# A two-turn engine loop written out, and a one-column sum of squares, in a fused hybrid block on one core

## The reference, cut to what matters

```python
x = x + attn_a(layernorm(x))   # gated recurrence over time, 8 heads, state 64 x 128 per head
x = x + ffn(layernorm(x))      # x @ ternary(weight).T * alpha + bias
x = x + attn_b(layernorm(x))   # softmax attention across the 8 sequences, 16 heads of 8
x = x + ffn(layernorm(x))      # the same weights as above
```

```python
y = y * rsqrt(mean(y * y, axis=-1) + 1e-6) * rms_weight     # y is 512 wide
return y @ out_proj_w.T
```

## Time and profile before

| what | us |
|---|---|
| median of 3 runs | 606.64 (604.37 to 607.63) |
| the profiled execution's own time | 608.52 |
| its span, from the first to the last instruction | 606.8 |
| mean granted TensorE clock in it | 0.966 of full speed |
| busy: PE, DVE, ACT, POOL | 526.3, 470.1, 482.5, 433.8 |

### The profile page before, as it was taken

How to read it: one execution, slowest core, us unless ns; L and a number is a source line. 1 busy time by engine, 2 the same in 40 slices (tenths; PEclk the granted TensorE clock), 3 DMA queues, 4 the chain that set the end, 5 groups by cost and what they waited for, 6 DMA issues and landing times. The chain is left out here.

```text
span 606.8 us, 13457 instructions
## 1 busy us (share of the span) xinstructions
PE 526.3 (87%) x3932; PEld 437.9 (72%) x3932; DVE 470.1 (77%) x1093; ACT 482.5 (80%) x1478; POOL 433.8 (71%) x568
## 2 busy tenths in 40 slices
PE   5978999999999898896999888899998786879287
PEld 4866888888887777785887777788777575766175
DVE  6666576687659999983767999997559979953995
ACT  3799999999998879695998887789999789843101
POOL 7348777878777887783678796977768876944742
PEclk9989999999999999997999999999999989987769
DMA  8841222132111112231111111232211112000001
GB/s 198 219 112 50 75 74 81 59 99 76 59 44 52 59 59 59 62 102 35 56 59 59 59 53 31 93 94 93 88 31 54 63 41 66 27 18 2 1 0 36
DMA packets 52309, 39.44 MB, mean 65 GB/s; under 512 B 7301, under 2 KB 48010, under 8 KB 52234
## 3 DMA queue, kind: packets, MB, share of 16 engines
q1 hardware_dynamic: 45898, 35.39, 19.7%
q10 hardware_dynamic: 6336, 3.15, 1.8%
HBM read 33.44 MB, written 4.46 MB: 62 GB/s over the span
## 5 line engine op out<-in xcount | busy, mean ns | idle before, releaser
L937 ACT ACTIVATE turned<-ps,sct 128x128 f32<-128x128 f32 x376 | 110.7, 446 | 0.0
L922 ACT ACTIVATE turned<-ps,sct 128x128 f32<-128x128 f32 x368 | 103.3, 434 | 6.4 <-DMA sct<-packed 3.9
L1282 DVE TENSOR_TENSOR_SCAN lmat<-arow,band 128x512 f32<-128x512 f32 x64 | 86.5, 1356 | 5.6 <-POOL band L651 3.6
L630 POOL TENSOR_TENSOR cn<-turned 128x256 f32<-128x256 f32 x64 | 54.4, 850 | 39.4 <-ACT turned L937 39.4
L1290 DVE TENSOR_TENSOR mmat<-ps,lmat 128x512 f32<-128x512 f32 x64 | 43.9, 685 | 46.4 <-PE ps L1816 46.4
L630 POOL TENSOR_TENSOR bn<-turned 128x256 f32<-128x256 f32 x64 | 52.9, 826 | 36.7 <-PE ps L1848 25.1
L1816 PE MATMUL ps<-cT,bT 128*128 128x128 f32 x512 | 69.4, 278 | 8.2 <-DVE state L1321 5.8
L1816 PEld LDWEIGHTS ps<-cT,bT 128*128 128x128 f32 x512 | 63.2, 191 | 16.4 <-issue 14.9
L828 ACT ACTIVATE area<-ps 128x256 f32<-128x256 f32 (+1 forms) x68 | 34.6, 565 | 42.8 <-PE ps L2049 14.0
L1721 PE MATMUL ps<-w_sel_hi,xt_hi 128*128 128x512 f32 x128 | 59.1, 462 | 1.4 <-ACT turned L937 1.4
L1848 PE MATMUL ps<-wu,bn 128*128 128x128 f32 x384 | 54.6, 286 | 4.0 <-DVE mmat L1290 3.9
(11 more groups left out here) (271 smaller groups left out, 1430.1 us busy)
## 6 DMA issues: line engine op xcount, KB each, us to landing
arow<-alpha_rows SPq DMA_DIRECT2D x32, 512.0 KB, 3.7
drow<-decay_rows SPq DMA_DIRECT2D x64, 128.0 KB, 3.1
area<-in_L_attn_a_x_dram SPq DMA_DIRECT2D x4, 512.0 KB, 6.1
xT_rows<-turned SPq DMA_DIRECT2D x4, 512.0 KB, 4.9
xt<-xT_rows SPq DMA_DIRECT2D x32, 64.0 KB, 2.5
area<-in_L_attn_a_x_dram ACTq DMA_DIRECT2D x6, 256.0 KB, 3.0
out_dram<-area ACTq DMA_DIRECT2D x6, 256.0 KB, 2.4
area<-L_attn_a_sel_proj_w_dram SPq DMA_DIRECT2D x2, 512.0 KB, 6.4
```

Of the source, the lines that this page charges most:

```text
L630: pool.tensor_tensor(out[:, 0], zc[:, 0], zs[:, 1], ALU.subtract)
L922: last = act.activation(dst[h][:, N * q:N * q + N], bank(BK_B)[:, N * q:N * q + N], ACT.Copy, scale=scalars(c, k)[:, at + HH * h + q:at + ...
L937: last = act.activation(dst[h][:, N * q:N * q + N], bank(BK_C)[:, N * q:N * q + N], ACT.Copy, scale=scalars(c, k)[:, at + HH * h + q:at + ...
L1282: dve.tensor_tensor_scan(lmat[h], arow[i2][:, HH * P * h:HH * P * (h + 1)], band[h], 0.0, ALU.mult, ALU.add).then_inc(l_dve, 1)
```

## The change

The loop of each engine over chunks 1 and 2 becomes a loop of the program text, so that all 16 units stand twice in each engine's instruction stream, and c is a number there. And the product of `ysum` with a matrix of ones, which gave the same sum in 128 columns, takes one column of ones and writes one column.

```diff
@@ run_chunks
-    with eng.Fori(1, NC - 1) as c:
+    for c in range(1, NC - 1):
         for k in range(UNITS):
             step(c, k, pieces)
@@ SP's program
-            with sp.Fori(1, NC - 1) as c:
+            for c in range(1, NC - 1):
                 for b in range(NB):
                     tile_loads(c, b)
@@ project_out
-                pe.matmul(bank(BK_M)[:, D:2 * D], ysum[:], ones[:], start=True, stop=True).then_inc(o_pe, 1)
+                pe.matmul(bank(BK_M)[:, D:D + 1], ysum[:], ones[:, 0:1], start=True, stop=True).then_inc(o_pe, 1)
```

## The result

| | before | changed |
|---|---|---|
| median | 605.79 us (4 runs, 604.37 to 607.63) | 597.72 us (4 runs, 597.06 to 597.96) |
| profiled execution | 608.52 us, span 606.8 | 597.60 us, span 595.8 |
| mean granted clock in it | 0.966 | 0.968 |

The ratio is 0.9867, with a 95% interval of 0.9837 to 0.9897: faster by 1.3%, or 8.1 us.

A forecast was written before the change was run, and what follows sets the result against it. No engine fills the span; ScalarE paces chunk 0, and the loop's two equal turns have a stall between them. Terms of 8.27 + 0.31 + 0.2 + 0.2 - 0.4 = 8.6 us off 606.64 gave 598.0 us, 8-in-10 range 594.5 to 601.3.

The forecast's parts named there:

- The jump back: Between the loop's two turns, unit 31's scores to unit 32's: written out, the stall goes, saving 8.27 us.
- The entry: Where the loop starts: without the table load there, TensorE's way from L1829 to the next scores shortens by 0.31 us.
- The table's new place: ScalarE's exponential table loads right ahead of the first exponential, at 199.83 us before; cost 0.4 us, range 0 to 1.28.
- Registers: The loop's waits worked out in registers on TensorE's sequencer: 0.2 us saved, bounds 0 and 2.2 us.
- The one-column product: The sum of squares on TensorE, one column instead of 128: 0.2 us saved, with 0 and 5.3 us as ends.
- the clock at 1.00 from chunk 0 to past 480 us: Sign of being right: TensorE's granted clock stays full over that stretch; no size given.
- the low clock moves elsewhere in chunks 1 and 2: Sign of being wrong: TensorE's half clock shows up at another place in those chunks; no size given.
- The sum: Total over the whole kernel: 8.27 + 0.31 + 0.2 + 0.2 - 0.4 = 8.6 us saved.
- The stall stays: Rival, chance 0.04: late streams come from the amount of program text passed, so straight text stalls somewhere too; 606 us.
- Given back: Rival, chance 0.05: chunk 2's units come 8 us earlier, then a transfer or VectorE holds them; 602 or 603 us.
- Table loads multiply: Rival, chance 0.02: each of 6 exponentials up to chunk 3 brings two table loads on ScalarE; 608 to 613 us.
- Columns count: Rival, chance 0.05: the narrower sum saves 0.17 us on each of 24 tiles, all on the path; 594 us.

The follow-up runs named there:

- loop on TensorE alone: The changed kernel, but TensorE keeps its loop of two turns while the other engines stay written out: 606.78 us, ratio 1.0020 to the kernel before.
- two loops without a jump back: The changed kernel with chunks 1 and 2 each in a hardware loop of one turn on every engine: 597.75 us, ratio 0.9866 to the kernel before.
- text only: The changed kernel with the 128-column sum of squares put back, loops still written out: 598.07 us, ratio 0.9888 to the kernel before.

## Why the prediction was right, and where it was not

The forecast was 598.0 us, and the median is 597.72. By its own steps:

- *The jump back, 8.27 us.* Right, and it is the whole of the gain. The step from unit 31 to 32 went from 16.15 to 7.89 us, 8.26 by these rows and -8.28 in the account by units from 24 to 32. That the cost is TensorE's taken jump and no other thing of the loop was argued from two branch durations, and is now shown: loop on TensorE alone 16.97 us, two loops without a jump back 7.88 us. That the units would not give it back held: -8.3 to -8.4 us up to unit 43.
- *The entry, 0.31 us.* By the stretch that the prediction priced, from L1829 to the next scores, 5.56 us became 5.25: 0.31 us. From unit 15 to 16 it is 0.17 us.
- *The table's new place, 0.4 us.* 0.29 us at unit 23, at the place and with the single load that were foreseen. The load began at 198.92 us and did not wait for the exponential's semaphore.
- *Registers, 0.2 us.* 0.0 us between units 24 and 31, registers and column together. All of it was hidden in that stretch. No experiment took the registers alone away. The upper bound of 2.2 us counted the largest group only; TensorE's sequencer has 104 ALU and 8 fused operations in all.
- *The one-column product, 0.2 us.* This is the step that failed, and in sign. The stream gains nothing, 0.334 us for 0.335 us over three starts; that end of the range was the right one. But the sum also had to say what a shorter record does to the clock, and the prediction named "the clock at 1.00 from chunk 0 to past 480 us" as a sign that it was right. The clock fell at 371.1 us, and the prediction's own sign of being wrong, that "the low clock moves elsewhere in chunks 1 and 2", came true. By the profiles above the fall behind the narrow sum takes 1.0 us in the changed kernel and 0.4 us in the least of the six, so this part of the change is a loss where the clock falls. The medians don't resolve it: text only 598.07 us, changed 597.72.
- *The sum.* 8.26 + 0.31 - 0.29 + 0 - 1.0 = 7.3 us by the stretches, against 8.6 forecast and 8.1 by the medians. The remaining 0.8 us lies within the measurement: the before's runs alone spread by over 3 us with the clock. So the mechanism of the large term was right, and that the total is within 0.3 us is partly luck: two small terms that were too hopeful, 0.4 us together, and the missed 1.0 us are less than what the measurement can tell.

The rivals. *The stall stays*: no idle with "issue" of over 1 us is left between 268 and 285 us. *Given back*: 1.0 us was, but by the clock and not by a transfer or VectorE. *Table loads multiply*: one load. *Columns count*: 0.0 us.

The profile held a hint. Before, PE waited 1.88 us at unit 43 at full clock. The prediction read that stretch only as a window mean, 1.00, and never asked how near each wait stood to a fall when the record in front of it was made shorter.

## What to carry to other kernels

A hardware loop whose body is long costs at each jump back, most of all on TensorE, where the clock falls behind the idle. The length to look at is an engine's own number of instructions: GpSimd's 246 cost nothing, VectorE's 438 cost it 2 us. A loop of one turn cost nothing here, and the registers of the loop of two turns were hidden. Price the jump by the stretch across it against the same work without it, and not by the branch's duration, which here was 3.8 of 8.3 us. On a TensorE that waits two microseconds now and then, a product made shorter may only bring the wait forward, and a few identity products put into the wait may be worth more; that is indicated here, not shown.

## What the runs showed that was not expected

- The taken jump over 16 units held TensorE's sequencer 3808 ns (5032 with the loop on TensorE alone), with a second idle time of 2.3 to 2.9 us two records on; over 4 products it took 232 ns at most, and GpSimd's over 246 instructions held nothing up. Each of TensorE's two idle times has a 16,384-byte packet of its instruction queue in it. The Trainium skill (Advanced Engine Details and Errata, Control Flow Timing) gives 108 ns for a compare-and-branch; the branches that fell through, 67 to 93 ns, are near that, the taken one over the long body is not.
- A product with one moving column, with new weights each time, starts its second record 30 ns after the first and pays it back: 0.334 us over three starts, 0.335 with 128 columns.
- The sum's two records, over in 0.39 us with 128 columns and in 0.28 us with one, made a difference to whether the clock fell behind a wait of 2 us at unit 43 of the straight text: with one column in 6 of 6 profiles, with 128 in none of 3, and with one column and seven identity products in the wait in none of 2. At unit 27 it fell behind one column in 2 of 8.
